# One count for both halves of a recurrent state: TensorE's two waits in each step of an RNN and mixture-of-experts kernel become one

## What is computed

```python
def step(prev_h, xw_t):
    next_h = jnp.tanh(xw_t + prev_h @ Wh)        # Wh 256 x 256, prev_h 2 x 256
    return (next_h, next_h)
_, hs = jax.lax.scan(step, h0, jnp.swapaxes(xW, 0, 1))      # 1024 steps
...
logits = x_flat @ gate_w.T                        # 2048 tokens, 8 experts
top_v, top_i = jax.lax.top_k(logits, 2)
...
hidden = jax.nn.silu(x_flat @ wge.T) * (x_flat @ wue.T)     # inner size 1024
acc + we[:, None] * (hidden @ wde.T)
```

## Time and profile before

| | us |
|---|---|
| median of 3 runs | 938.45 (937.93 to 940.91) |
| the profiled execution | 938.1 |
| its span, first to last instruction | 936.3 |
| PE busy (weight loads 668.3) | 785.4 |
| ACT busy | 480.5 |
| DVE busy | 443.5 |
| POOL busy | 137.9 |

### The profile page before, as it was taken

The page is one execution under the profiler, slowest core; times in us unless marked ns, Lnnn a source line. Parts: engine busy times, 40 slices in busy tenths (PEclk is TensorE's granted clock), DMA queues, the critical chain, the costliest instruction groups (busy, mean ns, idle before and its releaser), DMA issues.

```text
span 936.3 us, 42989 instructions
## 1 busy us (share of the span) xinstructions
PE 785.4 (84%) x17106; PEld 668.3 (71%) x17106; DVE 443.5 (47%) x2572; ACT 480.5 (51%) x2839; POOL 137.9 (15%) x134
## 2 busy tenths in 40 slices
PE   6454454799999999999989999999999999998795
PEld 4343343677787787778778777778778778888794
DVE  4666667353444444343444445353444434344552
ACT  4766767454544455454544545454544545454443
POOL 1000001002020201102020111212020111113323
PEclk7555555699999999999999999999999999897998
DMA  4666666301110111111111111111011111101121
GB/s 131 180 191 170 184 174 176 117 20 26 20 29 17 34 17 28 24 20 26 21 31 20 26 21 28 23 26 26 15 31 20 23 29 22 20 16 32 30 32 22
DMA packets 35635, 49.09 MB, mean 52 GB/s; under 512 B 5713, under 2 KB 22097, under 8 KB 35409
## 3 DMA queue, kind: packets, MB, share of 16 engines
q1 hardware_dynamic: 27200, 36.53, 14.3%
q0 software_dynamic: 7968, 9.58, 7.1%
q10 hardware_dynamic: 272, 0.26, 0.1%
HBM read 35.57 MB, written 12.88 MB: 52 GB/s over the span
## 4 chain that ended last, share of the span: by engine, by line
PE 77%; issue 8%; DVE 6%; ACT 6%; DMA 1%; another core or an unknown queue 1%; POOLq 0%; ACTq 0%; DVEq 0%
PE bank L470 36%; PE bank L593 23%; PE bank L615 11%; DVE state L1171 5%; ACT bank L840 4%; PE bank L624 2%; PE bank L452 1%; PE bank L572 1%; PE bank L564 1%; DMA arena<-w_all 1%; PE bank L690 1%; ACT w_hi L826 1%; DVE w_lo L1146 1%; PE bank L533 0%
## 5 line engine op out<-in xcount | busy, mean ns | idle before, releaser
L1171 DVE TENSOR_TENSOR state<-bank,state 128x4 f16<-128x4 f32 x1024 | 166.4, 163 | 443.3 <-ACT bank L840 426.9
L840 ACT ACTIVATE bank<-bank 128x4 f32<-128x4 f32 x1024 | 161.8, 158 | 400.0 <-PE bank L470 394.0
L470 PE MATMUL bank<-state,wh_hi 128*128 128x4 f16 (+1 forms) x4204 | 252.8, 165 | 131.4 <-DVE state L1171 111.9
L470 PEld LDWEIGHTS bank<-state,wh_hi 128*128 128x128 f16 x4204 | 190.7, 98 | 240.1 <-ACT state L832 185.7
L470 PE MATMUL bank<-state,wh_lo 128*128 128x2 f16 x4096 | 247.0, 164 | 0.3 <-issue 0.3
L470 PEld LDWEIGHTS bank<-state,wh_lo 128*128 128x128 f16 x4096 | 178.8, 97 | 0.9
L832 ACT ACTIVATE state<-bank 128x4 f16<-128x4 f32 x1024 | 174.6, 171 | 2.8 <-PE bank L470 2.7
L593 PE MATMUL bank<-x_T,w_hi 128*128 128x128 f16 (+1 forms) x1856 | 155.5, 207 | 3.5 <-issue 1.9
L615 PE MATMUL bank<-arena,w_hi 128*128 128x128 f16 (+1 forms) x1600 | 142.3, 210 | 0.7 <-issue 0.7
L593 PE MATMUL bank<-x_T,w_lo 128*128 128x128 f16 (+1 forms) x928 | 138.8, 207 | 0.0
L593 PE MATMUL bank<-arena,w_hi 128*128 128x128 f16 (+1 forms) x1344 | 132.8, 215 | 2.5 <-issue 1.6
(11 more groups left out here) (141 smaller groups left out, 1027.8 us busy)
## 6 DMA issues: line engine op xcount, KB each, us to landing
arena<-w_all SPq DMA_DIRECT2D x96, 256.0 KB, 2.9
xrow<-expert_rows SPq DMA_DIRECT2D x82, 66.0 KB
early<-xT SPq DMA_DIRECT2D x17, 128.0 KB
expert_rows<-pad SPq DMA_DIRECT2D x8, 132.0 KB, 3.0
expert_rows<-rows,slot POOLq DMA_INDIRECT x64
out<-y_sb,place_wide POOLq DMA_INDIRECT x30
out<-y_sb,place_now POOLq DMA_INDIRECT x20, 3.1
arena<-wh_in ACTq DMA_DIRECT2D x1, 256.0 KB, 4.1
```

What stands on the lines that cost most here:

```text
L470: return pe.matmul(out, w[:, k, m * P:(m + 1) * P], moving, start=False, stop=False, skip_group_check=True)
L840: act.activation(h32_at(n), preact(n), ACT.Tanh, scale=1 / SCALE).then_inc(s_h32, 1)
L1171: v.tensor_tensor(lo[:, i, :, B * tt:B * tt + B], h32_at(n).rearrange("p (c b) -> p c b", c=2), hi[:, i, :, B * tt:B * tt + B], ALU.subtra ...
```

## The change

The low half of the state and the early high half count on one semaphore, `s_next`. `made_before(n)` says how many of both have been made when step n may begin. PE waits for it once in each step; the first step alone also waits for the high halves made ahead of the loop, which stay on `s_hi`. The wait in `low_weights` goes, and the two waits after the loop become one. With `s_hi` no longer counted in the loop, the scatters' release moves to `s_h32`: to the full tanh of step `at` - 2, where it was the early half made in step `at` - 4.

```diff
-        s_lo = sem("h_lo")
+        s_next = sem("h_lo_and_early_h_hi")
...
+        def made_before(n):
+
+            return n - FIRST + 1 + min(n, N - LEAD) - FIRST
...
             def state_products(n):
 
                 leads = n + LEAD < N
-                pe.wait_ge(s_hi, min(n + LEAD, N) - FIRST + 1)
-                pe.wait_ge(s_lo, n - FIRST + 1)
+                if n == FIRST:
+                    pe.wait_ge(s_hi, LEAD + 1)
+                pe.wait_ge(s_next, made_before(n))
...
             def low_weights(n):
 
-                pe.wait_ge(s_hi, n - FIRST + 1)
...
             g = NBLK - 1
-            pe.wait_ge(s_hi, T + 1)
-            pe.wait_ge(s_lo, T + 1)
+            pe.wait_ge(s_next, made_before(N))
...
-            def hi_of(n):
+            def hi_of(n, made):
...
-                act.activation(hi[:, i, :, c:c + B], src, ACT.Tanh, scale=1 / SCALE).then_inc(s_hi, 1)
+                act.activation(hi[:, i, :, c:c + B], src, ACT.Tanh, scale=1 / SCALE).then_inc(made, 1)
...
                 if n + LEAD < N:
-                    hi_of(n + LEAD)
+                    hi_of(n + LEAD, s_next)
...
-                hi_of(n)
+                hi_of(n, s_hi)
...
-                                hi[:, i, :, B * tt:B * tt + B], ALU.subtract).then_inc(s_lo, 1)
+                                hi[:, i, :, B * tt:B * tt + B], ALU.subtract).then_inc(s_next, 1)
...
                 if at is not None:
-                    pool.wait_ge(s_hi, at - FIRST + 1)
+                    pool.wait_ge(s_h32, at - FIRST - 1)
```

More of the change, by code:

```diff
@@ L1219, in _ @@
             v.wait_ge(s_hi, 1)
-            v.tensor_tensor(lo[:, 0, :, R - B:R], h0[:], hi[:, 0, :, R - B:R], ALU.subtract).then_inc(s_lo, 1)
+            v.tensor_tensor(lo[:, 0, :, R - B:R], h0[:], hi[:, 0, :, R - B:R], ALU.subtract).then_inc(s_next, 1)
             v.wait_ge(s_gate, 32)
```

## The result

The changed kernel takes 873.19 us (median of 4 runs, 872.37 to 874.38), against 938.19 for the kernel before; the ratio is 0.930, with a 95% interval of 0.928 to 0.932. The forecast was 877.5. The profiled execution's span is 870.6 us where it was 936.3: 65.7 less.

The account below looks back on a forecast made before the run. Bound: a ring of three engines, with PE's separate wait in each turn. Saving 76.2 - 6.9 - 3.7 - 3.9 - 0.7 = 61.0 us takes 938.1 to 877.1, 877.5 as median; range 862 to 893.

Parts of the forecast that it names:

- The ring and its bound: Each of 1024 steps loops through ScalarE, VectorE and PE, 0.78 us; a riding wait saves 0.077 us, 76.2 in all.
- Rival 1: At PE's weight load: only the load comes earlier, not the matmul spacing behind it; 0.06 us a turn, 890 us; chance 0.12.
- Rival 4: At PE's wait: the single wait is still built as its own instruction, only the scatters move; 938 us; chance 0.03.
- PE's queue: PE's own work within a step is not the bound: 0.22 us free now, 0.14 left at a 0.700 us turn.
- The holds: POOL's indirect DMAs delay PE's hand-over to ScalarE until about 1.34 us after their start; loses 6.9 (adds) and 3.7 us (scatters).
- The other losses: Steps where VectorE's routing or a product ends late can't shrink, 3.9 us; first-stage weight loads landing late, 0.7 us.
- The weight chunks: First stage: weight transfers take 2.9 us to land, 4.2 at most, against cover shrinking to 3.5; 0.7 us lost.
- the scatters' later landing: Scatters released two steps later still land before the next pair's rows are needed; 0, up to 1.4 us a block otherwise.
- 990 of them: Recurrence: some 30 of the 1024 steps don't wait at PE in this form, so 990 x 0.077 = 76.2 us.
- 3 (the holds begin behind the hand-over): At POOL's indirect DMAs: delays start after the hand-over at the new phase; 855 to 866 us; chance 0.08.
- 5 (a second hand-over is caught): At POOL's DMAs: the shorter turn lets each delay a second hand-over, about one whole turn; slower, 951 us at 0.9; chance 0.02.
- The signs named for a right forecast: In the trace: no separate PE wait after the first steps, load 0.05 to 0.06 behind, turn 0.70, add's tanh at 1.34.

Follow-up runs that it names:

- the two runs on the waits: Kernel before with its two PE waits in the other order: ratio 0.935; changed kernel with a long met wait kept ahead of the common one: ratio 0.9965.
- the swap: Kernel before with PE's two waits in the other order, low half first, both semaphores kept: ratio 0.935, 884.0 us beside 944.0.
- the release at the matmuls: Changed kernel with each scatter let go by the state matmuls of the same step instead of a full tanh: ratio 0.9255, 867.7 us beside 938.3.
- the added scatters: Changed kernel with one more indirect scatter of 64 rows by POOL for each of 33 pairs, to a spare place: ratio 0.947.

## Why the prediction was right

**The ring and its bound**: right. The turn lost 77 ns (by the stamps in ns, 778 to 701 from tanh to tanh, median), of which 63 lie ahead of the load and 14 in the tighter start of the matmuls. Rival 1 had only the first; the example from an idle PE held in a loaded one too. Rival 4 is out by the timeline: the single wait rides with no other ahead of it, so the reason given for this rival doesn't hold. (Its price leaves out the scatters' 4 us, too.) What the two runs on the waits show is that the wait given first rides and the later one becomes an instruction of its own, and the kernel before had given the wrong one first. That was not in the forecast: I took the one count as the means, when a swap of two lines gives nearly all of it.

One reading was too wide. "Between 501.47 and 501.59 nothing computes" is true of the ring alone. PE's filler matmul, which started ahead of the gap, runs in it, and so does an instruction of VectorE's routing:

```profile
501.38 0.22 PE L624 MATMUL bank<-wh_hi 128*128 128x128 f16 x1
501.49 0.16 DVE L1029 SCALAR_TENSOR_TENSOR upto<-taken,have 128x2 f32<-128x2 f32 x1
```

That the filler isn't what the load waited for is shown by the changed kernel, where the load comes 0.07 ahead of the filler's end (481.11 and 481.18).

**PE's queue**: right. 0.15 us lie between the last start and the load where 0.14 were forecast; the last wide matmul's own 0.055 has still to come off both. The rule of the Trainium skill that was weighed ("TensorE: Matmul & The Clock Gate", "Back-to-back issue gap", 81 ns for each matmul of 128 columns) doesn't hold for this stream: its wide matmuls start 0.055 us apart in both traces, and PE fits its step into 0.70 us. The other one, that dense increments from several engines can deadlock another engine ("VectorE: DVE Perf Modes", "The TRN2 errata"), didn't show either, with both increments on one semaphore.

**The holds**: right in kind, somewhat small in size. Summed over the trace, the tanhs that come late behind POOL's DMAs cost 33.9 us before and 46.7 after, 12.8 more; the terms were 6.9 + 3.7. (Each sum has one tanh in it that comes 2.1 us late near the recurrence's end, in both kernels alike; its cause isn't known.) The adds cost 5.8 more (forecast 6.9; their hold ended 0.04 sooner behind the DMA than before), the scatters 5.9 (forecast 3.7; their hold ended 0.03 later), the few adds of 64 rows 1.1, which had no term. So the hold's end is not as fixed as "about 1.34" has it: its medians run from 1.33 to 1.52 over the kinds of DMA, kernels and chips.

**The other losses**: wrong in sign. The forecast took 3.9 us for turns that can't shrink and 0.7 for the weight chunks. From the full tanh to the low half's end the turns grew by only 1.9 us in sum, and the delays between low half and fourth matmul shrank, from 13.1 to 9.2. One reason could be that PE's sequencer sent its own wait behind a full queue, so that this wait and the dispatch after it were late. That is argued and not shown. The other traces speak against taking the whole of it for the change: where the wait met last stands alone the same delays sum to 12.9 and 13.4 us, where it rides to anything from 8.3 to 13.8, and 13.8 is the swap. The weight chunks and the scatters' later landing cost nothing that can be seen.

**The sum.** Each turn can be cut at the end of the low half and at the end of the state matmuls. Summed over the 1023 turns of each trace:

| from, to | before, us | after, us | difference |
|---|---|---|---|
| full tanh's start, low half's end | 362.4 | 364.3 | +1.9 |
| low half's end, state matmuls' end | 409.4 | 326.9 | -82.4 |
| state matmuls' end, next full tanh | 75.5 | 88.6 | +13.1 |

That is the whole 67.4 us. The 82.4 are 1023 x 0.077 = 78.8 and the delays that shrank. Against the forecast, all turns gained the 0.077, not 990 of them (2.6 us more). The other losses turned into a gain (6.4 us more). The holds took 2.5 us more than forecast, the stage behind the recurrence 1.5, and the start 0.2. Together that is 4.8; the spans give 65.7 against 61.0, 4.7. So the errors partly cancelled, and that the sum came within 4.3 us of the median is luck in part.

The 1.5 us of the last stage need not belong to the change: over all twelve traces it took 78.3 to 80.7 us, and its three longest (80.4 to 80.7) have the three lowest granted clocks, 0.90. Here the clock was 0.93 before and 0.91 after.

**The rivals**: 3 (the holds begin behind the hand-over) and 5 (a second hand-over is caught) did not happen in the changed kernel. Rival 5's mechanism is real, though: with the release at the matmuls one DMA does catch two hand-overs, at 0.13 + 0.14 us, not at a whole turn. The signs named for a right forecast all came: no separate wait, the load 0.05 to 0.06 behind the low half, 0.70 from tanh to tanh, and the add's tanh at 1.34 with 0.78 of idle time ahead of it.

## What to carry to other kernels

Where an engine waits for two semaphores ahead of one instruction, look in the trace for which of the waits stands as an instruction of its own, and let it be the one that is met first. In these kernels that means giving the wait that is met last first; merging counts does the same only because it leaves one wait. In a ring of dependent engines, every event with a fixed distance to something outside the ring takes the gain back at each meeting: count these events before you multiply a saving by the number of turns. Where such an event can be moved within the turn, try it, since it costs one line: here it gave 1.3% more.

## What the runs showed of the hardware

- Of several waits ahead of one instruction, the one given first rode on it and the later one became an instruction of its own (both orders, 1024 times each). When the wait met last stood alone on PE, the load came 0.12 us after the release; when it rode, 0.06, and the matmuls gained another 0.014 us. On POOL an indirect DMA started 0.76 us after its release with the wait met last standing alone, 0.28 with it riding.
- An indirect DMA of POOL holds PE's counts. A hand-over to ScalarE that is ready between about 0.64 and 1.3 us after the DMA's start passes mostly at 1.32 to 1.50 us (up to 1.67 for the added scatters), whether the instruction takes 0.9 us (scatters) or 1.6 (adds). One that is ready between 0.42 and 0.64 passes at once, or near 0.6, or only with the others. The count itself is late (by 0.38 us before, 0.47 after, medians); ScalarE starts 23 ns after it as always. Counts of ScalarE and VectorE showed no such delay.
- The same rows as a plain transfer of POOL, or POOL's fills, hold nothing. The first data packets of a scatter start 1.46 to 1.51 us after the DMA and those of an add 2.14 at the soonest, when the hold has long begun, so it isn't the transfer's traffic.
- There are exceptions. Some adds of 64 rows held nothing (in the kernel before, with a hand-over ready at 0.91), nor did most scatters of the first stage, where PE has little to do and its granted clock was 0.50 to 0.56. Near the recurrence's end some hand-overs ready at 0.42 were held to 1.3. Why, and what inside POOL's indirect DMA stops PE's counts, stays open.
